# Two-layer convolution attention: half of layer 0's probability tiles turned by VectorE and DRAM instead of TensorE

## The chip, the cores and the metric

The kernel runs on one core of one Trainium2 chip. The metric is the device time of one execution in microseconds; the number given for a kernel is the median of its runs. Engines are named as in the profile: PE is TensorE, DVE VectorE, ACT ScalarE, POOL GpSimd, SP the SyncE that issues all DMAs here.

## The reference

Four images `x` of 256 channels and 32x32 = 1024 positions, all f32. Two layers:

```
# layer 0, per image; xf is (256, 1024)
Bm, Cm, Dm = Wb @ xf, Wc @ xf, Wd @ xf
S   = softmax(Bm.T @ Cm, axis=-1)          # 1024 x 1024
y   = gamma * (Dm @ S.T) + x
# layer 1, per image, 4 heads of 64 channels
hn  = group_norm(y, 32 groups) * g + b
q, k, v = Wq @ hn + bq, Wk @ hn + bk, Wv @ hn + bv
out = y + Wp @ (softmax(q.T @ k / 8) @ v, all heads) + bp
```

Products are made in split form: an operand is held as a rounded `_hi` part and the rest `_lo`, and a product is three matmuls (hi*hi, lo*hi, hi*lo), or two where one side is stacked.

## The kernel before

The instruction stream of every engine is written out by hand; semaphores join them. Each engine works strictly in its own order.

Layer 0 runs image by image: `image0(i, last)` on each engine, three times in a loop and once more written out for the last image (which also carries the group norm of layer 1's first image). `Wb.T @ Wc` is folded beforehand into `wbc`, so that `a = wbc.T x` and scores are `a.T x`. An image has 8 tiles of 128 queries (`T0_IMAGE = 8`), step s = 0..7. In a step:

- PE (`scores0`): 12 matmuls of 512 columns into `scores[:, s % 2]`. It waits until the exponential of tile s - 2 has left that buffer.
- DVE (`row_max`): the negated row maximum. ACT (`exp`): the exponential into `prob[:, s % 2]` and the row sum. DVE (`recip`), then POOL (`normalise`): the probabilities, in place in `prob`.
- Two steps later (`LAG = 2`) PE (`transpose_tile`) turns the tile: eight 128x128 transposes into the PSUM buffer `trans`, two halves of four. ACT (`trans_high`) copies each half rounded into `pt_hi`, DVE (`trans_low`) subtracts it from `trans` into `pt_lo`. There is one `trans` buffer, so a tile's transposes wait for `pt_lo` of the tile before (semaphore `pt_split`).
- In the steps of `D_STEPS` PE (`project_d`) also makes a quarter of Dm transposed, a "d product" of 12 matmuls of 256 columns, into one of two `acc` banks; ACT (`high`) and DVE (`low`) empty it into `d_hi`, `d_lo`. DVE does its part one step later, after that step's row maximum. A third d product needs the bank of the first, and so on.

After step 7 PE waits for the last d product to be emptied (`evacuated(plan.number("d3"))`) and starts the value products, `av0` to `av3`, 24 matmuls each. av0 and av1 need the turned tiles 0 to 3 (half 0 of `pt_hi`, `pt_lo`), av2 and av3 tiles 4 to 7. The list `TAIL0` sets what lies between: the transposes t6 and t7 and the next image's `a` products. The last image has `TAIL0_LAST`, with layer 1's first q and k products. SP loads `y_out` (the residual x) and the next image's `x_raw` at the start of an image, in the last image `y_in` in place of `x_raw`, and stores `y_out` in the tail.

Layer 1 has 32 tiles per image with the same helpers; its work does not change.

## Time and profile before

| | us |
|---|---|
| median of 3 runs | 707.8 (707.26 to 708.27) |
| the profiled execution | 707.9 |
| its span | 705.8 |
| PE busy | 697.6 |
| DVE busy | 536.4 |
| ACT busy | 454.3 |
| POOL busy | 229.4 |

The profile shows one execution. Layer 0 fills the span from about 16 to 265 us, some 62 us for each of its four images; before it stand the weights, behind it layer 1. An image's steps 0 to 7 take a little over half of its time, the tail the rest. Rows of the timeline give the start, the duration and the idle time ahead of an instruction with what ended it. A row's duration is a few hundredths of a microsecond, on PE 0.16, longer than the distance to the next row on the same engine, because instructions overlap at their ends; in sums over a queue the distance counts.

### The profile page before, as it was taken

Reading aid. Unit: us, or ns where it says so; the run is one execution under the profiler, and the core shown is the slowest. Engines: PE = TensorE matmul, PEld = TensorE weight load, DVE = VectorE, ACT = ScalarE, POOL = GpSimd, SP = SyncE. Lnnn points to the kernel's source line nnn. Section 1 sums busy time; section 2 is a strip of 40 time slices with the busy share of each in tenths; the row PEclk is TensorE's granted clock in tenths of the full one; section 3 lists DMA queues with packets and bytes.
Section 4 is the critical chain, followed back from the end, with each engine's and each line's share of the span. In section 5 each row is a group of like instructions: output and inputs, shape, how many; then the busy total and the mean of one; then the engine's idle time right before and its main releaser. Section 6 shows DMA issues by size and latency. Waiting matters only on the chain.

```text
span 705.8 us, 11728 instructions
## 1 busy us (share of the span) xinstructions
PE 697.6 (99%) x3924; PEld 595.8 (84%) x3924; DVE 536.4 (76%) x876; ACT 454.3 (64%) x820; POOL 229.4 (33%) x216
## 2 busy tenths in 40 slices
PE   8999999999999999999999999999999999999997
PEld 7888888888888888888888888888988888888886
DVE  4665365456547738899888899888889988889996
ACT  5552254145226516889777779777778878778884
POOL 0220121022013303466333446434356533334431
PEclk9999999999999999999999999999999999999999
DMA  8000310040030175500357301265401155401001
GB/s 276 8 2 38 101 41 15 30 134 0 31 127 22 43 182 125 160 1 1 76 135 176 93 31 31 53 158 134 134 15 45 45 124 123 126 16 46 1 31 59
DMA packets 29096, 52.69 MB, mean 75 GB/s; under 512 B 3456, under 2 KB 5760, under 8 KB 29056
## 3 DMA queue, kind: packets, MB, share of 16 engines
q1 hardware_dynamic: 29056, 52.19, 26.8%
q8 instruction: 21, 0.34, 0.2%
q14 instruction: 19, 0.16, 0.1%
HBM read 18.62 MB, written 8.39 MB: 38 GB/s over the span
## 4 chain that ended last, share of the span: by engine, by line
PE 91%; DVE 4%; ACT 3%; issue 1%; DMA 0%; DVEq 0%; SPq 0%; ACTq 0%
PE acc L1125 46%; PE scores L1125 27%; PE trans L1159 18%; DVE negmax L796 2%; ACT prob L601 1%; DVE pt_lo L814 1%; ACT pt_hi L611 1%; DMA wc_raw<-in_wc 0%; PE trans L1171 0%; DVE o_sum L1028 0%; DVE rsum L801 0%; ACT o_sum L717 0%; DVE y_res L1037 0%; DVE wb_lo L886 0%; DVE qk L931 0%
## 5 line engine op out<-in xcount | busy, mean ns | idle before, releaser
L510 POOL TENSOR_SCALAR prob<-prob,rsum 128x1024 f32<-128x1024 f32 x159 | 179.2, 1127 | 428.4 <-DVE rsum L801 428.4
L611 ACT ACTIVATE pt_hi<-trans 128x512 fp32r<-128x512 f32 x320 | 174.4, 595 | 129.1 <-PE trans L1159 128.6
L796 DVE TENSOR_REDUCE negmax<-scores 128x1 f32<-128x1024 f32 x160 | 194.3, 1214 | 44.3 <-PE scores L1125 43.3
L814 DVE TENSOR_TENSOR pt_lo<-trans,pt_hi 128x512 fp32r<-128x512 f32 x320 | 204.6, 680 | 7.0 <-ACT pt_hi L611 6.6
L601 ACT ACTIVATE prob<-scores,negmax 128x1024 f32<-128x1024 f32 x160 | 179.1, 1119 | 30.1 <-DVE negmax L796 28.5
L1159 PEld LDWEIGHTS trans<-ident,prob 128*128 128x128 f32 x1280 | 147.5, 140 | 26.8 <-issue 3.8
L1159 PE MATMUL trans<-ident,prob 128*128 128x128 f32 x1280 | 167.7, 273 | 1.3 <-DVE pt_lo L814 1.1
L1125 PE MATMUL scores<-k_st,q_st 128*128 128x512 f32 x512 | 137.7, 391 | 0.0
L1125 PEld LDWEIGHTS scores<-k_st,q_st 128*128 128x128 f32 x512 | 95.8, 188 | 20.4
L1125 PE MATMUL acc<-pt_hi,v_st 128*128 128x512 f32 (+1 forms) x264 | 106.8, 407 | 0.6 <-DVE pt_lo L814 0.6
L1125 PE MATMUL acc<-pt_lo,v_st 128*128 128x512 f32 (+1 forms) x264 | 101.0, 385 | 0.0
L1125 PEld LDWEIGHTS acc<-pt_hi,v_st 128*128 128x128 f32 x264 | 49.8, 189 | 7.8 <-DVE pt_lo L814 0.8
L1125 PEld LDWEIGHTS acc<-pt_lo,v_st 128*128 128x128 f32 x264 | 50.0, 189 | 7.1
L1125 PE MATMUL scores<-x_hi,a_hi 128*128 128x512 f32 x128 | 50.8, 397 | 0.0
L1125 PE MATMUL acc<-pt_hi,d_hi 128*128 128x512 f32 x128 | 50.7, 396 | 0.0
L1125 PE MATMUL scores<-x_hi,a_lo 128*128 128x512 f32 x128 | 50.0, 391 | 0.0
L1125 PE MATMUL scores<-x_lo,a_hi 128*128 128x512 f32 x128 | 49.9, 390 | 0.0
L1125 PE MATMUL acc<-pt_hi,d_lo 128*128 128x512 f32 x128 | 49.9, 390 | 0.0
L1125 PE MATMUL acc<-pt_lo,d_hi 128*128 128x512 f32 x128 | 49.9, 390 | 0.0
L801 DVE RECIPROCAL rsum<-rowsum 128x1 f32<-128x1 f32 x160 | 25.7, 161 | 27.0 <-ACT prob L601 22.3
L626 ACT ACTIVATE a_hi<-acc 128x512 fp32r<-128x512 f32 x16 | 9.6, 598 | 46.7 <-PE acc L1125 46.7
L945 DVE SCALAR_TENSOR_TENSOR y_out<-acc,vec,y_out 128x512 f32<-128x512 f32 x16 | 12.0, 750 | 27.6 <-PE acc L1125 27.6
(121 smaller groups left out, 892.7 us busy)
## 6 DMA issues: line engine op xcount, KB each, us to landing
k_st<-qk SPq DMA_DIRECT2D x64, 256.0 KB, 4.7
q_st<-qk SPq DMA_DIRECT2D x64, 128.0 KB, 2.4
x_raw<-in_x SPq DMA_DIRECT2D x8, 512.0 KB, 6.9
y_out<-in_x SPq DMA_DIRECT2D x16, 256.0 KB, 3.6
y_scratch<-y_out SPq DMA_DIRECT2D x16, 256.0 KB, 2.0
y_in<-y_scratch SPq DMA_DIRECT2D x4, 1024.0 KB, 7.2
y_res<-y_scratch SPq DMA_DIRECT2D x16, 256.0 KB, 3.8
out<-y_res SPq DMA_DIRECT2D x16, 256.0 KB, 2.1
```

The lines of the kernel that those rows point to most:

```text
L510: nc.gpsimd.tensor_scalar(p, p, rsum[:, t % 2:t % 2 + 1], 1.0, ALU.mult, ALU.mult)\
L601: nc.scalar.activation(prob[:, t % 2, :], scores[:, t % 2, :], ACT.Exp, bias=negmax[:, t % 2:t % 2 + 1], scale=1.0, accum_out=rowsum[:, t ...
L611: nc.scalar.activation(pt_block(pt_hi, (t // 4) % 2, t, h), trans[:, h, :].rearrange("p (j n) -> p j n", n=P), ACT.Copy).then_inc(pt_high, 1)
L626: nc.scalar.activation(dst, acc[:, plan.bank(name), :], ACT.Copy).then_inc(acc_high, 1)
L796: nc.vector.tensor_reduce(negmax[:, t % 2:t % 2 + 1], scores[:, t % 2, :], AX_X, ALU.max, negate=True).then_inc(max_ready, 1)
L801: nc.vector.reciprocal(rsum[:, t % 2:t % 2 + 1], rowsum[:, t % 2:t % 2 + 1]).then_inc(rsum_ready, 1)
L814: nc.vector.tensor_tensor(pt_block(pt_lo, slot, t, h), trans[:, h, :].rearrange("p (j n) -> p j n", n=P), pt_block(pt_hi, slot, t, h).bitc ...
L945: nc.vector.scalar_tensor_tensor(y_out[:, a, :], acc[:, plan.bank(f"av{a}"), :], vec[:, GAMMA:GAMMA + 1], y_out[:, a, :], ALU.mult, ALU.ad ...
L1125: ins = nc.tensor.matmul(dst, w, m, start=(starts and n == 0), stop=(stops and n == len(pairs) - 1))
L1159: ins = nc.tensor.transpose(trans[:, h, b * P:(b + 1) * P], prob[:, t % 2, j * P:(j + 1) * P], ident[:, :])
```

## The change

In layer 0, tiles 0 to 3 of every image (`TURNED = 4`) are no longer turned by PE. DVE (`turn`) transposes the normalised tile in 32x32 blocks from `prob` into one of three `turned` buffers, sorting the blocks by column on the way; SP stores it to DRAM (`store_turned`) and reads it back with the blocks of rows exchanged (`load_turned`, four DMAs of 32 rows), right into `pt_lo`. ACT (`turn_high_of`) then rounds the whole tile of 128x1024 from `pt_lo` into `pt_hi`, and DVE (`turn_low_of`) subtracts in place. Tiles 4 to 7 go as before. Half 0 of `pt_hi`, `pt_lo` now has another order of keys, which `turned_keys` gives to av0 and av1. The d products move from steps 1, 2, 4, 5 to 3, 4, 5, 6. The exponential of tiles 2 to 5 now waits for the turn of two tiles before instead of for PE's transposes. In step 4, DVE turns tile 3 ahead of the row maximum; in steps 1 to 3 the turn comes behind it.

The diff, cut; index changes of the semaphore counts (`TR_IMAGE`, `TR_SHIFT`) are left out:

```diff
-D_STEPS = [1, 2, 4, 5]
+D_STEPS = [3, 4, 5, 6]
+TURNED = 4
+TURN_SLOTS = 3
+TURN_HIGH = {4: [0], 5: [1, 2], 6: [3]}
+TURN_LOW = {4: [0], 5: [1], 6: [2, 3]}
...
 # SP, image0
+            def store_turned(i, t):
+                sp.wait_ge(turn_ready, TURNED * i + t + 1)
+                sp.dma_start(turn_dram[t], turned[:, t % TURN_SLOTS, :]).then_inc(turn_stored[t % TURN_SLOTS], 16)
+            def load_turned(i, t):
+                sp.wait_ge(turn_stored[t % TURN_SLOTS], turns_stored(i, t) + 16)
+                blocks = turn_dram[t].rearrange("(q c) (g n) -> g c q n", q=QUADS, g=QUADS)
+                for g in range(QUADS):
+                    rows = turned_tile(pt_lo, t).bitcast(F32)[g * QUAD:(g + 1) * QUAD, :]
+                    sp.dma_start(rows.rearrange("c (q n) -> c q n", q=QUADS), blocks[g]).then_inc(turn_moved[t], 16)
...
                     load_x(i + 1)
+                for t in range(TURNED):
+                    store_turned(i, t)
+                    if t > 0:
+                        load_turned(i, t - 1)
+                load_turned(i, TURNED - 1)
...
 # ACT, image0
+            def turn_high_of(i, t):
+                act.wait_ge(turn_moved[t], TURN_DMA * (i + 1))
+                nc.scalar.activation(turned_tile(pt_hi, t), turned_tile(pt_lo, t).bitcast(F32), ACT.Copy)\
+                    .then_inc(turn_high, 1)
...
                 for s in range(T0_IMAGE):
-                    if s >= LAG:
+                    if s >= LAG + TURNED:
                         trans(s - LAG)
-                    exp(t0, s)
+                    exp0(i, s)
...
                         high(d_part(d_hi, n), plan, f"d{n}")
+                    for t in TURN_HIGH.get(s, []):
+                        turn_high_of(i, t)
...
 # DVE, image0
+            def turn(i, t):
+                dve.wait_ge(prob_ready, T0_IMAGE * i + t + 1)
+                dve.wait_ge(turn_stored[t % TURN_SLOTS], turns_stored(i, t))
+                nc.vector.transpose(turned[:, t % TURN_SLOTS, :],
+                                    prob[:, t % 2, :].rearrange("p (j g c) -> p g j c", g=QUADS, c=QUAD))\
+                    .then_inc(turn_ready, 1)
+            def turn_low_of(i, t):
+                dve.wait_ge(turn_high, TURNED * i + t + 1)
+                nc.vector.tensor_tensor(turned_tile(pt_lo, t), turned_tile(pt_lo, t).bitcast(F32),
+                                        turned_tile(pt_hi, t).bitcast(F32), ALU.subtract).then_inc(turn_low, 1)
...
                         recip(t0, s - 1)
+                    if s == TURNED:
+                        turn(i, s - 1)
                     row_max(t0, s)
+                    if 1 <= s < TURNED:
+                        turn(i, s - 1)
                     if s - 1 in D_STEPS:
...
-                    if s >= LAG:
-                        trans_low(t0, s - LAG)
+                    if s >= LAG + TURNED:
+                        trans_low(TR_IMAGE * i - TURNED, s - LAG)
+                    for t in TURN_LOW.get(s, []):
+                        turn_low_of(i, t)
...
 # PE, image0
-                        pe.wait_ge(pt_split, SPLIT_CREDIT + 2 * t0 + 8 * (half + 1))
+                        if half == 0:
+                            pe.wait_ge(turn_low, TURNED * i + TURNED)
+                        else:
+                            pe.wait_ge(pt_split, SPLIT_CREDIT + 2 * TR_IMAGE * i + 2 * TR_IMAGE)
```

What stands in a row on the engines that wait for each other. First DVE in the loop over images, from the reciprocal that opens step 5, as it was (`exp_ready`, `scores_ready` and `acc_high` are the semaphores of the exponential, the scores and the d product's copy):

```order
L801 RECIPROCAL rsum<-rowsum 128x1 [waits exp_ready]
L796 TENSOR_REDUCE negmax<-scores 128x1 [waits scores_ready]
L897 REGISTER_ALU
L898 TENSOR_TENSOR d_lo<-acc,d_hi 128x512 [waits acc_high]
L812 ISA
L814 TENSOR_TENSOR pt_lo<-trans,pt_hi 128x4x128 [waits pt_high]
```

And now, steps 4 and 5:

```order
L870 RECIPROCAL rsum<-rowsum 128x1 [waits exp_ready]
L882 ISA [waits prob_ready]
L883 STREAM_TRANSPOSE turned<-prob 128x1024 [waits turn_stored0]
L865 TENSOR_REDUCE negmax<-scores 128x1 [waits scores_ready]
L980 REGISTER_ALU
L981 TENSOR_TENSOR d_lo<-acc,d_hi 128x512 [waits acc_high]
L889 ISA
L890 TENSOR_TENSOR pt_lo<-pt_lo,pt_hi 128x1024 [waits turn_high]
L870 RECIPROCAL rsum<-rowsum 128x1 [waits exp_ready]
L865 TENSOR_REDUCE negmax<-scores 128x1 [waits scores_ready]
```

The turn of tile 3 stands ahead of the maximum of step 4, and the subtraction of turned tile 0, which waits for ACT, ahead of the maximum of step 5.

ACT in step 4, before:

```order
L610 REGISTER_ALU
L611 ACTIVATE pt_hi<-trans 128x4x128 [waits transposed]
L599 REGISTER_ALU
L600 ISA [waits max_ready]
L601 ACTIVATE prob,rowsum<-scores,negmax 128x1024 [waits transposed]
L596 REGISTER_ALU
L626 ACTIVATE d_hi<-acc 128x512 [waits acc_done]
```

And now, in step 4 and at the start of step 5 (`turn_moved0` is counted up by the four loads of tile 0):

```order
L655 REGISTER_ALU [waits max_ready]
L668 ACTIVATE prob,rowsum<-scores,negmax 128x1024 [waits turn_ready]
L645 REGISTER_ALU
L693 ACTIVATE d_hi<-acc 128x512 [waits acc_done]
L663 ISA
L664 ACTIVATE pt_hi<-pt_lo 128x1024 [waits turn_moved0]
L653 REGISTER_ALU
L655 REGISTER_ALU [waits max_ready]
```

The copies out of `trans` ahead of the exponential are gone, and a copy of twice the width stands behind the d product's.

DVE from step 7 to the tail, before (`res_loaded` opens the tail's first result):

```order
L801 RECIPROCAL rsum<-rowsum 128x1 [waits exp_ready]
L796 TENSOR_REDUCE negmax<-scores 128x1 [waits scores_ready]
L812 ISA
L814 TENSOR_TENSOR pt_lo<-trans,pt_hi 128x4x128 [waits pt_high]
L812 REGISTER_ALU
L814 TENSOR_TENSOR pt_lo<-trans,pt_hi 128x4x128 [waits pt_high]
```

And now, from the end of step 6:

```order
L890 TENSOR_TENSOR pt_lo<-pt_lo,pt_hi 128x1024 [waits turn_high]
L870 RECIPROCAL rsum<-rowsum 128x1 [waits exp_ready]
L865 TENSOR_REDUCE negmax<-scores 128x1 [waits scores_ready]
L980 REGISTER_ALU
L981 TENSOR_TENSOR d_lo<-acc,d_hi 128x512 [waits acc_high]
L895 ISA
L897 TENSOR_TENSOR pt_lo<-trans,pt_hi 128x4x128 [waits pt_high]
```

The emptying of the last d product, for which PE waits ahead of av0, has come behind the maximum of step 7; it was in step 6.

## Rows read from the trace of the kernel before

**Rows 1.** Page, part 1: busy us, share of the span, instructions.

```profile
PE 697.6 (99%) x3924; PEld 595.8 (84%) x3924; DVE 536.4 (76%) x876; ACT 454.3 (64%) x820; POOL 229.4 (33%) x216
```

**Rows 2.** Timeline of PE, second image: start us, us, engine, line, what.

```profile
78.45 0.39 PE L1125 MATMUL scores<-x_hi,a_hi 128*128 128x512 f32 x1
...
83.89 0.28 PE L1125 MATMUL acc<-wd_hi,x_hi 128*128 128x256 f32 x1
...
85.32 0.40 PE L1125 MATMUL scores<-x_hi,a_hi 128*128 128x512 f32 x1
...
93.14 1.03 PE L1159 MATMUL trans<-ident,prob 128*128 128x128 f32 x8
...
96.75 1.03 PE L1159 MATMUL trans<-ident,prob 128*128 128x128 f32 x8
...
111.27 0.48 PE L1125 MATMUL acc<-pt_hi,d_hi 128*128 128x512 f32 x1
```

**Rows 3.** Timeline of DVE, the same image.

```profile
81.37 1.22 DVE L796 TENSOR_REDUCE negmax<-scores 128x1 f32<-128x1024 f32 x1 [1.40 <-PE scores L1125]
83.95 0.17 DVE L801 RECIPROCAL rsum<-rowsum 128x1 f32<-128x1 f32 x1 [1.35 <-ACT prob L601]
...
89.42 0.68 DVE L898 TENSOR_TENSOR d_lo<-acc,d_hi 128x512 fp32r<-128x512 f32 x1
90.01 1.28 DVE L814 TENSOR_TENSOR pt_lo<-trans,pt_hi 128x512 fp32r<-128x512 f32 x2
91.21 0.15 DVE L801 RECIPROCAL rsum<-rowsum 128x1 f32<-128x1 f32 x1
```

**Rows 4.** Timeline of ACT, the same image.

```profile
82.71 1.11 ACT L601 ACTIVATE prob<-scores,negmax 128x1024 f32<-128x1024 f32 x1 [3.46 <-DVE negmax L796]
...
89.68 1.12 ACT L601 ACTIVATE prob<-scores,negmax 128x1024 f32<-128x1024 f32 x1
...
90.77 0.61 ACT L626 ACTIVATE d_hi<-acc 128x512 fp32r<-128x512 f32 x1
```

**Rows 5.** Timeline of POOL, the same image.

```profile
91.56 1.12 POOL L510 TENSOR_SCALAR prob<-prob,rsum 128x1024 f32<-128x1024 f32 x1 [3.41 <-DVE rsum L801]
```

**Rows 6.** Groups by form: busy us, mean ns; idle before. All operands in SBUF.

```profile
L892 DVE TENSOR_TENSOR x_lo<-x_raw,x_hi 128x1024 fp32r<-128x1024 f32 x8 | 9.5, 1223 | 1.0 <-ACT x_hi L622 0.5
L622 ACT ACTIVATE x_hi<-x_raw 128x1024 fp32r<-128x1024 f32 x8 | 8.1, 1058 | 0.2 <-DMA x_raw<-in_x 0.2
L807 DVE TENSOR_SCALAR prob<-prob,rsum 128x1024 f32<-128x1024 f32 x1 | 0.8, 754 | 0.0
```

**Rows 7.** SP's issues, a window with DMA share and GB/s last, landing times.

```profile
81.09 1.94 SPq L423 DMA_DIRECT2D y_out<-in_x  x4
83.30 0.94 SPq L390 DMA_DIRECT2D x_raw<-in_x  x2
...
91.00:92.00 1.00, 1.00 (x7) 0.80 (x5) 0.36 (x2) 0.38 (x1) 0.44 (x1) 1.00 0.04 16
...
q_st<-qk SPq DMA_DIRECT2D x64, 128.0 KB, 2.4
```

**Rows 8.** Timelines of PE, POOL, ACT and DVE in the last image.

```profile
202.26 0.39 PE L1125 MATMUL scores<-x_hi,a_hi 128*128 128x512 f32 x1
...
235.57 0.48 PE L1125 MATMUL acc<-pt_hi,d_hi 128*128 128x512 f32 x1
...
212.12 1.35 POOL L538 TENSOR_TENSOR gn_root<-gn_var,minus_half 128x6 f32<-128x6 f32 x1
...
223.74 0.64 ACT L661 ACTIVATE h_hi<-y_in 128x512 fp32r<-128x512 f32 x1
...
215.51 0.29 DVE L868 TENSOR_TENSOR gn_scale<-gn_root,vec 128x2 f32<-128x2 f32 x3
...
228.05 0.68 DVE L355 TENSOR_TENSOR h_lo<-y_in,h_hi 128x512 fp32r<-128x512 f32 x1
```

**Rows 9.** Timeline of PE at the program's start.

```profile
1.81 4.64 PE L1171 MATMUL trans<-ident 128*128 128x128 f32 x20 [1.81 <-POOL ident L490]
```

More of the change, by code:

```diff
@@ L53 @@
 FIRST_A = ["a0", "a1", "a2", "a3"]
-D_STEPS = [1, 2, 4, 5]
+D_STEPS = [3, 4, 5, 6]
+TURNED = 4
+TR_IMAGE = T0_IMAGE - TURNED
+TR_SHIFT = IMAGES * TURNED
+QUAD = 32
+QUADS = P // QUAD
+TURN_SLOTS = 3
+TURN_DMA = QUADS * 16
+TURN_HIGH = {4: [0], 5: [1, 2], 6: [3]}
+TURN_LOW = {4: [0], 5: [1], 6: [2, 3]}
 TAIL0 = ["av0", "t6", ("av1", 0, 2), "t7", ("av1", 1, 2), "av2", "next_a0", ("av3", 0, 3), "next_a1",
@@ L315, in build @@
         transposed = sem("transposed")
+        turn_ready = sem("turn_ready")
+        turn_stored = [sem(f"turn_stored{n}") for n in range(TURN_SLOTS)]
+        turn_moved = [sem(f"turn_moved{n}") for n in range(TURNED)]
+        turn_high = sem("turn_high")
+        turn_low = sem("turn_low")
         pt_high = sem("pt_high")
@@ L363, in flat, with turned_tile, turned_keys, turns_stored @@
             return ap.rearrange("p a b -> p (a b)")
+        def turned_tile(buf, t):
+            return buf[:, 0, :, :].rearrange("p j n -> p (j n)")[:, t * N:(t + 1) * N]
+        def turned_keys(buf, j):
+            return buf[:, 0, :, :].rearrange("p j n -> p (j n)").rearrange("p (m j c) -> p m j c", j=NT, c=QUAD)[:, :, j, :]
+        def turns_stored(i, t):
+            return FREE_CREDIT + 16 * (2 * i + t // TURN_SLOTS if t % TURN_SLOTS == 0 else i)
         def pt_block(buf, half_slot, t, h):
@@ L381, in _ @@
         def _(sp):
-            for s in (y_stored, out_stored, *qk_stacked):
+            for s in (y_stored, out_stored, *qk_stacked, *turn_stored):
                 sp.sem_inc(s, FREE_CREDIT)
@@ L599, in exp, with exp0, exponential @@
                 act.wait_ge(max_ready, t0 + t + 1)
-                act.wait_ge(transposed, TRANS_CREDIT + 2 * (t0 + t) - 2)
+                act.wait_ge(transposed, TRANS_CREDIT + 2 * (t0 - TR_SHIFT + t) - 2)
+                exponential(t)
+            def exp0(i, t):
+                act.wait_ge(max_ready, T0_IMAGE * i + t + 1)
+                if 2 <= t < 2 + TURNED:
+                    act.wait_ge(turn_ready, TURNED * i + t - 1)
+                else:
+                    tiles = TR_IMAGE * i + (t - TURNED if t >= 2 + TURNED else t)
+                    act.wait_ge(transposed, TRANS_CREDIT - 2 + 2 * tiles)
+                exponential(t)
+            def turn_high_of(i, t):
+                act.wait_ge(turn_moved[t], TURN_DMA * (i + 1))
+                nc.scalar.activation(turned_tile(pt_hi, t), turned_tile(pt_lo, t).bitcast(F32), ACT.Copy)\
+                    .then_inc(turn_high, 1)
+            def exponential(t):
                 nc.scalar.activation(prob[:, t % 2, :], scores[:, t % 2, :], ACT.Exp,
@@ L609, in trans_high @@
                 for h in range(2):
-                    act.wait_ge(transposed, TRANS_CREDIT + 2 * (t0 + t) + h + 1)
+                    act.wait_ge(transposed, TRANS_CREDIT + 2 * (tr + t) + h + 1)
                     nc.scalar.activation(pt_block(pt_hi, (t // 4) % 2, t, h),
@@ L669, in trans @@
                     before = BASES["layer0"] + len(LAYER0) * (i - 1) + LAYER0.index("av3" if t >= 4 else "av1")
-                    trans_high(t0, t, before)
+                    trans_high(TR_IMAGE * i - TURNED, t, before)
                 for s in range(T0_IMAGE):
-                    if s >= LAG:
+                    if s >= LAG + TURNED:
                         trans(s - LAG)
-                    exp(t0, s)
+                    exp0(i, s)
                     if last and s - 1 in NORM_STEPS0:
@@ L766, in image1 @@
                         evacuate(plan, head_outputs(STEPS1[s]), i)
-                    trans_high(t1, s, before)
+                    trans_high(t1 - TR_SHIFT, s, before)
                     if s + LAG < T1_IMAGE or not plan.last:
@@ L1148, in over_k, with transpose_tile @@
                         for pair in products((w(0, k), m(0, k)), (w(1, k), m(1, k)))]
-            def transpose_tile(t0, t, last=False):
+            def transpose_tile(t0, tr, t, last=False):
                 if last and t >= T1_IMAGE - DVE_TILES:
@@ L1249, in values @@
                     if ct == 0 and part == 0:
-                        pe.wait_ge(pt_split, SPLIT_CREDIT + 2 * t0 + 8 * (half + 1))
+                        if half == 0:
+                            pe.wait_ge(turn_low, TURNED * i + TURNED)
+                        else:
+                            pe.wait_ge(pt_split, SPLIT_CREDIT + 2 * TR_IMAGE * i + 2 * TR_IMAGE)
+                    keys = (lambda buf, j: buf[:, 1, j, :]) if half else turned_keys
                     group(plan, f"av{n}", [
                         pair for j in range(NT)
-                        for pair in products((d_hi[:, j, col(ct, P)], pt_hi[:, half, j, :]),
-                                             (d_lo[:, j, col(ct, P)], pt_lo[:, half, j, :]))],
+                        for pair in products((d_hi[:, j, col(ct, P)], keys(pt_hi, j)),
+                                             (d_lo[:, j, col(ct, P)], keys(pt_lo, j)))],
                         part=part, parts=parts)
@@ L1374, in image1 @@
                         side_values(0, 0, 2)
-                    transpose_tile(t1, s, plan.last)
+                    transpose_tile(t1, t1 - TR_SHIFT, s, plan.last)
                     if not (plan.first and s == 0) and not groups_first:
```

25 lines of the change are left out of this document (13 added, 12 removed).

## Prediction

> **What bounds the kernel now.** I read the busy times first: PE is busy for 697.6 of 705.8 us, DVE for 76% and ACT for 64% [rows 1]. So what counts is which PE work goes, and whether DVE and ACT, now comfortably behind PE, can keep up where they get more. Then I read one image of layer 0 on PE [rows 2]: the reader is to see that its groups follow each other without a gap. Two score groups fill 78.45 to 83.89, so one takes 2.72 us; a d product takes 1.43 (83.89 to 85.32); from one tile's transposes to the next is 3.61 (93.14 to 96.75), which less 2.72 leaves 0.90 for the eight transposes of a tile. The first value matmul starts at 111.27, 32.8 us after the image's first score matmul. I call that stretch the head of an image and count its times from 78.45. Since PE never waits in it before, any change shows as the new start of av0 against 32.8; what follows av0 keeps its order, paced by PE. Last I read DVE, ACT and POOL in the same stretch for the hand-overs [rows 3 to 5]: scores done to row maximum 0.20 (81.17 to 81.37); maximum to exponential 1.34 (81.37 to 82.71); exponential to reciprocal 1.24 (82.71 to 83.95); reciprocal to POOL 0.35 (91.21 to 91.56), where normalising takes 1.12; exponential to the next ACT instruction 1.09 (89.68 to 90.77); d_lo 0.59 and a pt_lo pair 1.20 on DVE's queue (89.42, 90.01, 91.21). A PE that has run dry needs about 0.2 more to load weights. With these numbers the head before comes out at 32.9 by hand, the trace says 32.8.
>
> **What goes from PE.** Tiles 0 to 3 of each of four images lose 8 transposes: 4 x 0.90 = 3.6 us an image, 14.4 in all. If nothing else bound, the time would be 707.9 - 14.4 = 693.5.
>
> **The first steps, scores only.** With d products moved from steps 1, 2, 4, 5 to 3, 4, 5, 6, score groups 0 to 3 stand back to back. scores(2) needs exp(0): 2.72 + 0.20 + 1.34 + 1.24 + 0.23 = 5.73 against 5.44 when PE is free, so 0.3 us of waiting; scores(3) then just fits.
>
> **The turn on DVE.** The trace has no block transpose. Nearest rows of 128x1024 f32: 0.75 for the in-place scale from SBUF, 1.22 for the x_lo subtraction [rows 6]; a maximum over the same elements is 1.22 too [rows 3]. I take 1.22, or 1.14 on the queue, since an operation that moves every element once has no reason to be at the fast row's pace; I keep 0.75 and 2.44 (two passes) as ends. A step of DVE in this stretch is then recip 0.15 + max 1.14 + turn 1.14 = 2.4, which fits 2.72. But turn(3) is placed ahead of max(4): exp(3) starts at 12.7, recip(3) at 14.0, POOL works 14.3 to 15.4, turn(3) 15.5 to 16.7, so max(4) starts at 16.7, where scores(4) had been done at 15.5. That alone costs PE nothing, which has d(1), scores(5) and d(2) to do.
>
> The Trainium skill gives two figures here. "VectorE: DVE Perf Modes", The three transpose paths, has 311 ns for 128x128 on VectorE, by which eight blocks would be some 2.5 us, an estimate; "Vector Engine (DVE) Microarchitecture Reference", The reshape front-end and per-opcode configuration, says that a transpose sustains one element per cycle per lane, which is the pace of the rows at 1.22. No row here shows the operation; by the first figure the sum would be that of the first rival.
>
> **The hand-over that takes PE's place.** From step 4 on, each DVE step ends in turn_low, which waits for turn_high on ACT, which stands behind exp and d_hi of the same step, which wait for this step's maximum. The next maximum stands behind turn_low. So DVE and ACT go in a ring: max to exp 1.34, exp 1.09, d_hi 0.52, turn_high 1.09 (x_hi, same shape and source, 1.06 [rows 6]), turn_low 1.14 (x_lo, 1.22), recip 0.15: 5.33 us a step. PE needs 2.72 + 1.43 = 4.15 a step. Hence max(5) at 22.0, max(6) at 27.3. In step 6 DVE's own queue is the longer: max 1.14, d_lo(2) 0.60, pt_lo(4) 1.20, turn_low(2) and (3) 2.28, recip 0.15 = 5.37, so max(7) at 32.7. Only then comes d_lo(3), done at 34.5, and PE waits for it ahead of av0 (evacuated(d3)): av0 at 34.8. PE alone would have been there at 32.8 - 3.6 + 0.3 = 29.5. So 3.6 us of transposes go and 5.5 us of waiting come: in two pieces, some 2 us ahead of the transposes of tile 5 (their buffer waits for pt_lo(4)) and some 3 us ahead of av0. Net **+1.9 us** an image.
>
> **The round trip.** SP issues the store of a tile and later four loads; two x_raw issues take 0.94 and four y_out issues 1.94, so some 2 us of SP for a tile's four loads [rows 7]. The x loads of the next image are ahead in the same queue and still fill the DMA until about 91, 12.6 on our count; the window behind it is empty [rows 7]. Store(0), issued at 8.4, would land at 14 to 14.5, its loads be issued by 16.3 and land (128 KB: 2.4 us) near 18.7; turn_high(0) is due at 19.6. The later three have 2 to 4 us to spare. turn(3) also needs slot 0, stored by 14.5, due 15.5. So I cost the round trip at nothing, hidden behind exp(4) and the wait for POOL, with 1 us of cover; every microsecond that it is later than that is one on the ring. The y and x issues that follow on SP lie far ahead of need.
>
> **The last image** has group norm work in the same queues [rows 8]: the root on POOL (1.35) and the affine step on DVE (three rows of 0.29 at 0.33 apart and a copy, 1.1) now lie between turn(1) and recip(2), with no d product under them: max(4) comes 1.4 later. h_hi stands between exp and d_hi in steps 4 and 5: 2 x 0.52. h_lo stands in DVE's step 6: 0.60. Its head before was itself 33.3 (202.26 to 235.57), not 32.8: 0.5 less. 1.9 + 1.4 + 1.0 + 0.6 - 0.5 = **+4.4**.
>
> **Sum.** 3 x 1.9 + 4.4 = +10.1 us. The profiled execution took 707.9 us (span 705.8 and 2.1 around it), the median of the runs is 707.8; 707.9 + 10.1 = 718.0. Ends of the unknown: a turn of 0.75 takes some 0.4 off an image (716.5); 0.2 less on turn_high and turn_low together take off 0.6 (715.5); a round trip 1 us past its cover adds 1 (722), 3 us add 3 (some 728 to 730).
>
> **Rivals.** (A) *The turn takes two passes, 2.44.* Then DVE itself sets steps 1 to 3: recip 0.15 + max 1.43 with the wait for POOL + turn 2.36 = 3.94 a step, max(4) moves to 21.3 and the head by 6.5 us: 707.9 + 4 x 6.5 + 2.5 = about 736. Against it stand the rows at 1.22. (B) *DVE and ACT keep up, so that the kernel is faster.* Place: the ring of steps 4 to 6. It decides at the point where av0 can start by 32.8, 1.9 earlier than I have it: three turns of the ring at 4.7 instead of 5.33. If turn_high and turn_low went at half my durations each turn would lose 1.1 and the head would end at about 31.4: 707.9 - 4 x 1.4 + 2.5 = about 705; with the ring gone altogether 707.9 - 14.4 + 1.2 = 694.7. For it speaks that DVE is busy for only 76% of the span and ACT for 64% [rows 1]; against it that this is a chain of waits, not a load. (C) *The round trip is late.* Stores and loads share DMA queues with 2 MB of x traffic; if tile 0 lands 1 to 3 us after 19.6, 722 to 730. (D) *PE's clock falls in the pauses.* PE would stand for some 2 and 3 us with a short burst between. At the program's start 20 matmuls of 128 columns took 0.232 each, those of a transposed tile 0.13 [rows 9, 2]: the lower level costs as much again. If it held through av0 (5.4 us) that is at most 5.4 more an image, 739; I would give half of it, 728. No stretch of the trace has pauses of this size, for or against.
>
> **Chances.** Forecast 0.58 (715 to 721), A 0.10, B 0.09, of which two thirds beat the old kernel by over 0.2% and a third lies within it, C 0.17, D 0.06. The range takes in the forecast, most of C and D and the mild part of A: 713 to 729. Within 0.2% (1.4 us, about what a measurement of this kernel tells from no change) 0.03, faster 0.06, slower 0.91.
>
> **What would show it.** PE waits ahead of av0 for d_lo, about 3 us in each image, and ahead of tile 5's transposes about 2; DVE waits for turn_high about 2.3 us twice an image; maxima 4, 5, 6 of an image 5.3 apart; PE's busy time falls by some 14 us plus what is modelled in pauses; the block transpose has a row near 1.2. Wrong if ACT waits for the load of tile 0 (C), if transposes last over 1.5 (A), if the granted clock falls below 1.00 in a head (D), or if maxima come at PE's 4.15 (B).

## The result, and the profile after

The changed kernel takes 726.5 us (median of 4 runs, 725.53 to 727.14) against 707.9 (707.26 to 708.27) for the kernel before: 1.026 times as long, 95% interval 1.0252 to 1.0277. The direction was as forecast, and the time lies within the range of 713 to 729, but 8.5 us above the forecast of 718.0. The experiments are mostly about these 8.5 us.

The profiled execution took 727.1 us, with a span of 725.4 against 705.8. From the page of the changed kernel come the busy times, to be held against [rows 1], the row of PE's granted clock (tenths of full speed in 40 slices), one group of matmuls (busy us, mean ns, idle before it), and two rows of DMA issues (count, KB each, us from issue to landing):

```profile
PE 696.2 (96%) x3796; PEld 587.5 (81%) x3796; DVE 553.7 (76%) x876; ACT 453.7 (63%) x804; POOL 229.5 (32%) x216
...
PEclk9989999999899999999999999999999999999999
...
L1214 PE MATMUL acc<-pt_hi,d_hi 128*128 128x512 f32 x128 | 55.3, 432 | 14.9 <-DVE d_lo L981 14.9
...
turn_scratch<-turned SPq DMA_DIRECT2D x16, 512.0 KB, 4.4
pt_lo<-turn_scratch SPq DMA_DIRECT2D x64, 128.0 KB, 3.7
```

128 transposes are gone from PE, yet its busy time fell by only 1.4 us, not by the 14 that they took and that the prediction named as a sign. That is the first sign that the matmuls that stayed have become slower.

To find where the time is, I cut each image in two at the start of its first value matmul (av0). The head, as in the prediction, runs from the image's first score matmul to av0; I call what follows, up to the next image's first score matmul (or, behind the last image, layer 1's), the tail. All numbers are differences of start times on PE's timeline.

| us | image 0 | 1 | 2 | 3 | sum |
|---|---|---|---|---|---|
| head before | 32.82 | 32.82 | 32.82 | 33.31 | 131.8 |
| head after | 34.80 | 35.02 | 34.64 | 37.02 | 141.5 |
| tail before | 29.08 | 29.09 | 29.08 | 30.70 | 118.0 |
| tail after | 31.84 | 30.96 | 32.13 | 33.19 | 128.1 |

The heads grew by 9.7 us, where 10.1 was forecast. The tails, costed at nothing, grew by 10.2. What lies ahead of the first image became 0.4 shorter; its end stands between 16.0 and 16.9 us in the ten traces of this document, so 0.4 is within what it varies by. Layer 1's first score matmul comes 19.5 later (266.27 before, 285.76 after), and the span is 19.6 longer: layer 1 is untouched.

The second image's head, as DVE's and ACT's timelines show it (start us, us, engine, line, what; in brackets the idle time before it and who ended it):

```profile
98.38 1.25 DVE L883 STREAM_TRANSPOSE turned<-prob 128x1024 f32<-128x1024 f32 x1 [1.48 <-POOL prob L559]
99.54 1.19 DVE L865 TENSOR_REDUCE negmax<-scores 128x1 f32<-128x1024 f32 x1
...
103.56 1.23 DVE L890 TENSOR_TENSOR pt_lo<-pt_lo,pt_hi 128x1024 fp32r<-128x1024 f32 x1 [2.24 <-ACT pt_hi L664]
...
104.78 1.21 DVE L865 TENSOR_REDUCE negmax<-scores 128x1 f32<-128x1024 f32 x1
...
108.77 1.23 DVE L890 TENSOR_TENSOR pt_lo<-pt_lo,pt_hi 128x1024 fp32r<-128x1024 f32 x1 [2.19 <-ACT pt_hi L664]
...
109.98 1.21 DVE L865 TENSOR_REDUCE negmax<-scores 128x1 f32<-128x1024 f32 x1
...
115.79 1.21 DVE L865 TENSOR_REDUCE negmax<-scores 128x1 f32<-128x1024 f32 x1
116.92 0.68 DVE L981 TENSOR_TENSOR d_lo<-acc,d_hi 128x512 fp32r<-128x512 f32 x1
```

```profile
102.47 1.06 ACT L664 ACTIVATE pt_hi<-pt_lo 128x1024 fp32r<-128x1024 f32 x1
...
109.99 1.06 ACT L664 ACTIVATE pt_hi<-pt_lo 128x1024 fp32r<-128x1024 f32 x1 [1.25 <-DMA pt_lo<-turn_scratch]
```

The four maxima (tiles 4 to 7) stand 5.24, 5.20 and 5.81 us apart. Between the first two pairs DVE stands 2.2 us for ACT's half of the turned tile, which itself could start only behind this step's exponential. This is the ring of the prediction. Here is what it does to PE at the end of the head and just behind it; the windows under it hold, after the times, the busy us of PE, PEld, DVE, ACT and POOL, then the granted clock (third number from the end):

```profile
112.44 1.25 PE L1248 MATMUL trans<-ident,prob 128*128 128x128 f32 x8 [0.73 <-DVE pt_lo L897]
117.82 0.79 PE L1214 MATMUL acc<-pt_hi,d_hi 128*128 128x512 f32 x1 [4.12 <-DVE d_lo L981]
118.41 0.63 PE L1214 MATMUL acc<-pt_hi,d_lo 128*128 128x512 f32 x1
118.83 0.63 PE L1214 MATMUL acc<-pt_lo,d_hi 128*128 128x512 f32 x1
```

```profile
113.00:114.00 1.00, 0.70 (x5) 0.42 (x4) 1.00 (x1) 1.00 (x4) 0.00 (x0) 1.00 0.00 0
...
117.00:118.00 1.00, 0.18 (x1) 0.18 (x2) 1.00 (x2) 0.89 (x1) 0.20 (x1) 0.76 0.00 0
118.00:119.00 1.00, 1.00 (x3) 0.82 (x4) 0.86 (x3) 0.32 (x2) 0.00 (x0) 0.50 0.00 0
120.00:121.00 1.00, 1.00 (x4) 0.73 (x4) 0.00 (x0) 0.00 (x0) 0.18 (x1) 0.53 0.00 0
121.00:122.00 1.00, 1.00 (x6) 0.80 (x5) 0.00 (x0) 0.00 (x0) 0.00 (x0) 1.00 0.00 0
```

PE is still at its full 2.4 GHz (clock 1.00) when the pause of 4.12 us begins, and near its end the granted clock falls to 0.50, the 1.2 GHz level. When av0 starts, its matmuls of 512 columns follow each other at 0.42 to 0.43 us instead of 0.23. At about 121 the clock is back. In images 0, 2 and 3, with pauses of 3.57, 3.81 and 3.40 us ahead of av0, the granted clock is at 0.50 when av0 starts, too, and is back at about 56, 189 and 257 us, 5 to 6 us behind that start.

My theory after this reading had three parts: the heads are the ring and the late d_lo; most of the tails is the clock after the pause; and what is left of the tails is something in the matmuls themselves, since also at full clock they start 0.237 to 0.24 apart instead of 0.227. The rivals were that the tails are slow because data arrive late (the round trip, or POOL and DVE behind it), and that the heads wait for the round trip rather than for the ring.

### The profile page after: what moved, and what is told of

Its sections match the earlier page's. It is cut to its first block, busy times and chain, and to the rows that moved or that the text cites. A ratio compares the mean times of both kernels' runs of the same rounds, so it can differ in the third digit from the quotient of the medians.

```text
span 725.4 us, 11499 instructions
## 1 busy us (share of the span) xinstructions
PE 696.2 (96%) x3796; PEld 587.5 (81%) x3796; DVE 553.7 (76%) x876; ACT 453.7 (63%) x804; POOL 229.5 (32%) x216
## 4 chain that ended last, share of the span: by engine, by line
PE 74%; DVE 9%; ACT 5%; issue 5%; DMA 4%; POOL 1%; SPq 1%; DVEq 0%; ACTq 0%; POOLq 0%
PE acc L1214 43%; PE scores L1214 16%; PE trans L1248 15%; DVE negmax L865 4%; DMA turn_scratch<-turned 3%; ACT prob L668 2%; DVE pt_lo L897 1%; DMA pt_lo<-turn_scratch 1%; ACT pt_hi L678 1%; POOL prob L559 1%; SPq L461 1%; ACT pt_hi L664 1%; DVE turned L883 1%; DVE pt_lo L890 1%; DVE rsum L870 0%
## 5 line engine op out<-in xcount | busy, mean ns | idle before, releaser
L678 ACT ACTIVATE pt_hi<-trans 128x512 fp32r<-128x512 f32 x288 | 157.0, 595 | 99.8 <-PE trans L1248 99.3
L897 DVE TENSOR_TENSOR pt_lo<-trans,pt_hi 128x512 fp32r<-128x512 f32 x288 | 184.2, 681 | 10.8 <-ACT pt_hi L678 10.4
L1248 PEld LDWEIGHTS trans<-ident,prob 128*128 128x128 f32 x1152 | 132.3, 140 | 32.0 <-issue 6.5
L1248 PE MATMUL trans<-ident,prob 128*128 128x128 f32 x1152 | 152.0, 274 | 6.4 <-DVE pt_lo L897 5.5
L1214 PE MATMUL acc<-pt_hi,d_hi 128*128 128x512 f32 x128 | 55.3, 432 | 14.9 <-DVE d_lo L981 14.9
L1214 PE MATMUL acc<-pt_hi,d_lo 128*128 128x512 f32 x128 | 53.7, 420 | 0.0
L1214 PE MATMUL acc<-pt_lo,d_hi 128*128 128x512 f32 x128 | 53.4, 417 | 0.0
L1214 PEld LDWEIGHTS acc<-pt_hi,d_hi 128*128 128x128 f32 x128 | 26.3, 206 | 21.6 <-DVE d_lo L981 15.8
```

Of the source, the lines that this page charges most:

```text
L678: nc.scalar.activation(pt_block(pt_hi, (t // 4) % 2, t, h), trans[:, h, :].rearrange("p (j n) -> p j n", n=P), ACT.Copy).then_inc(pt_high, 1)
L897: nc.vector.tensor_tensor(pt_block(pt_lo, slot, t, h), trans[:, h, :].rearrange("p (j n) -> p j n", n=P), pt_block(pt_hi, slot, t, h).bitc ...
L1214: ins = nc.tensor.matmul(dst, w, m, start=(starts and n == 0), stop=(stops and n == len(pairs) - 1))
L1248: ins = nc.tensor.transpose(trans[:, h, b * P:(b + 1) * P], prob[:, t % 2, j * P:(j + 1) * P], ident[:, :])
```

## Experiment 1: give PE work in the pause

Where the image's PE program comes to its wait for the last d_lo, 12 matmuls are put in. They write into a score buffer that nobody reads any more.

```diff
+                pe.wait_ge(exp_ready, t0 + T0_IMAGE + 1)
+                for _ in range(12):
+                    nc.tensor.matmul(scores[:, 0, 0:H], a_hi[:, 0, 0:P], x_hi[:, 0, 0:H], start=True, stop=True)
```

> The changed kernel with 12 extra matmuls of 512 columns (2.7 us at full rate) that PE makes in the pause ahead of av0 into the scores buffer of tile 6, which nobody reads any more. The heads of the images (first score matmul to av0) should stay at 34.8 to 37.0 us. Theory 1 (about half of the loss, 10.2 of 19.5 us, is the granted clock that falls in the pause and comes back only inside av0 and av1): the granted clock stays at 1.00, the stretches from av0 to the next image's scores return from 31 to 32 us to 29.1, and the kernel takes 726.5 - 10.2 = 716 us. Rival (the values are slow for another reason, such as the other order of keys in their operands): the stretches stay at 31 to 32 us and the kernel at 726.

Measured: 718.9 us (718.47 to 719.23; 1.0155 times the kernel before on that chip, 1.0138 to 1.0172), 7.6 less than the change. PE's timeline of the second image:

```profile
111.47 3.01 PE L1375 MATMUL scores<-x_hi,a_hi 128*128 128x512 f32 x12
115.29 0.50 PE L1214 MATMUL acc<-pt_hi,d_hi 128*128 128x512 f32 x1 [0.81 <-DVE d_lo L981]
115.62 0.40 PE L1214 MATMUL acc<-pt_hi,d_lo 128*128 128x512 f32 x1
115.86 0.40 PE L1214 MATMUL acc<-pt_lo,d_hi 128*128 128x512 f32 x1
```

More work on PE makes the kernel faster. In sum the heads are what they were (34.79, 34.37, 34.38 and 37.82), so nothing arrives earlier; the tails fall to 29.57, 29.56, 29.56 and 30.91. The clock is thus worth 8.5 us of the tails (128.12 less 119.60), and late data none of them. Still 1.65 above the tails before remain, in matmuls 0.24 apart. They are the larger part of the 3 us by which 719 is above what I had expected; most of the rest is the last image's head of 37.8. Here is why it is longer than the 37.0 of the change, a row of PE's timeline and a window of the last image:

```profile
242.25 4.52 PE L1375 MATMUL scores<-x_hi,a_hi 128*128 128x512 f32 x12
...
243.00:244.00 1.00, 1.00 (x4) 0.81 (x3) 1.00 (x3) 0.23 (x1) 0.00 (x0) 0.50 0.00 0
```

In this image PE had already stood for 2.36 us ahead of the transposes of tile 5, and just behind them the granted clock fell to 0.50. The 12 extra matmuls took 4.4 us instead of the 2.9 of the second image, and av0 (246.61) had to wait for them. So the filler did not keep the clock up everywhere; here it took the slow stretch in av0's place.

## Experiment 2: turn_low a step later

If DVE waits for turn_high because it follows too closely, let it come one step later:

```diff
-TURN_LOW = {4: [0], 5: [1], 6: [2, 3]}
+TURN_LOW = {5: [0, 1], 6: [2, 3]}
```

> The changed kernel with the subtractions of turned tiles 0 and 1 one step later, so that TURN_LOW is 5: 0, 1 and 6: 2, 3; nothing else. Theory 1 (the ring of DVE and ACT: maximum, exponential, d copy, turned copy, subtraction, next maximum): maxima 4, 5, 6 come at PE's pace, the head falls from 34.8 to about 32.8 us, the pause ahead of av0 to under 3 us, and with it the clock stays up more often: 708 to 713 us. Rival (DVE is simply full from step 4 on, or PE waits for the late d copy whatever the order): the work on DVE is the same, so the head stays within 0.5 of 34.8 and the kernel at 724 to 727 us.

Measured: 719.6 us (718.99 to 720.69; 1.0171, 1.0154 to 1.0188), 7 less than the change but 7 to 12 more than I expected. In the first image the head falls to 32.6, as the theory of the ring says. In the second and third it is 34.3 and 34.4, only 0.8 and 0.3 less than in the change: here ACT waits for the turned tile itself, for 2.6 and 2.7 us of 6.6 in all. In the last it falls from 37.0 to 34.4. The clock accounts for much of the rest of the miss: it stays at 1.00 over the 2.42 us that PE stands ahead of av0 in the first image, and falls to 0.50 in the other three (4.25, 4.25 and 3.40 us), whose tails are 31.1, 30.8 and 33.7. The first row is from the list of waits (us in total, times, longest us), the second from ACT's timeline of the second image.

```profile
ACT pt_hi L664 <- DMA pt_lo<-turn_scratch: 6.6, 4, 2.7
...
105.49 1.06 ACT L664 ACTIVATE pt_hi<-pt_lo 128x1024 fp32r<-128x1024 f32 x1 [2.58 <-DMA pt_lo<-turn_scratch]
```

So with the ring loosened the round trip takes its place in the second and third image, less than 2 us behind it. The prediction's "hidden, with 1 us of cover" was right about the change and says nothing for a kernel that is 2 us quicker there.

## Experiment 3: the d products late, and nothing else

On the kernel before, only the steps of the d products are moved; all tiles are still turned by PE.

```diff
-D_STEPS = [1, 2, 4, 5]
+D_STEPS = [3, 4, 5, 6]
```

> The kernel before with only the d products moved to steps 3, 4, 5, 6; no tile is turned by DVE. Theory 1: d_lo(3) stands behind the maximum of step 7 and PE waits for it ahead of av0 by some 1.6 us an image, too short for the clock to fall: 707.9 + 4 x 1.6 = 714 us. Rival (the late d products are hidden and only the turned tiles cost): 708 us, within 1. A third: the pause brings the clock down here too: 720 us or more.

Measured: 714.7 us (714.20 to 715.42; 1.0100, 1.0083 to 1.0117), as expected; the heads are 34.5 to 34.9. Rows from DVE's and PE's timelines of the second image:

```profile
112.49 1.22 DVE L796 TENSOR_REDUCE negmax<-scores 128x1 f32<-128x1024 f32 x1 [1.97 <-PE scores L1125]
113.63 0.68 DVE L898 TENSOR_TENSOR d_lo<-acc,d_hi 128x512 fp32r<-128x512 f32 x1
```

```profile
114.53 0.49 PE L1125 MATMUL acc<-pt_hi,d_hi 128*128 128x512 f32 x1 [1.21 <-DVE d_lo L898]
114.86 0.40 PE L1125 MATMUL acc<-pt_hi,d_lo 128*128 128x512 f32 x1
```

The move costs 6.5 us by itself: the last d_lo stands behind the last maximum on DVE, and av0 waits for it. There is a pause ahead of av0 here too, of 1.21 us, and the granted clock stays at 1.00, with matmuls at the usual distance.

## Experiment 4: a new order of the steps

This keeps all that the change does and reorders it: the first d product back at step 1, the last at 5, turn_high early and turn_low late, and each turn behind the maximum of its step in tile 4's step too.

```diff
-D_STEPS = [3, 4, 5, 6]
+D_STEPS = [1, 3, 4, 5]
...
-TURN_HIGH = {4: [0], 5: [1, 2], 6: [3]}
-TURN_LOW = {4: [0], 5: [1], 6: [2, 3]}
+TURN_HIGH = {4: [0, 1], 5: [2], 6: [3]}
+TURN_LOW = {5: [0, 1], 6: [2, 3]}
...
-                    if s == TURNED:
-                        turn(i, s - 1)
...
-                    if 1 <= s < TURNED:
+                    if 1 <= s <= TURNED:
```

> The changed kernel in another order: d products in steps 1, 3, 4, 5, the turn of tile 3 behind the maximum of step 4, turned copies on ACT in steps 4 (tiles 0, 1), 5 (2), 6 (3), subtractions on DVE in steps 5 (0, 1) and 6 (2, 3). Theory 1: no ring, no maximum behind a subtraction that waits, d_lo(3) in step 6. By the same sum as in the prediction the head is 30.5 to 31.8 us, so 1.0 to 2.3 less than before an image, PE's pause under 2 us, the clock stays up: 699 to 705 us, faster than both kernels. Rival (the round trip through DRAM is the bound once the ring is gone): ACT waits for the loads in step 4, the head is 33 us or more and the kernel at 708 or above.

Measured: 708.5 us (706.57 to 709.88, 10 runs; 1.0003, 0.9993 to 1.0013). That is 18 us less than the change and no different from the kernel before, above the 699 to 705 that I expected and at the rival's time. In the first image the head is 30.8; in the others 32.3 to 32.7. First the row from the list of waits and one from ACT's timeline, then two from PE's and one window, all of the second image but the first:

```profile
ACT pt_hi L664 <- DMA pt_lo<-turn_scratch: 10.9, 8, 2.5
...
99.61 1.06 ACT L664 ACTIVATE pt_hi<-pt_lo 128x1024 fp32r<-128x1024 f32 x1 [2.27 <-DMA pt_lo<-turn_scratch]
```

```profile
105.74 1.25 PE L1246 MATMUL trans<-ident,prob 128*128 128x128 f32 x8 [0.46 <-DVE pt_lo L897]
108.88 0.50 PE L1212 MATMUL acc<-pt_hi,d_hi 128*128 128x512 f32 x1 [1.89 <-DVE pt_lo L890]
...
110.00:111.00 1.00, 1.00 (x4) 0.78 (x3) 1.00 (x2) 0.94 (x1) 0.15 (x1) 0.50 0.00 0
```

The maxima of tiles 4 to 6 start at 93.35, 97.53 and 101.92, so 4.2 and 4.4 us apart, close to PE's 4.15 a step: the ring is gone. The 18 us were thus the order, and now the round trip is what ACT waits for, 8 times. SP's issues show why the first image, with a head of 30.8, fares better:

```profile
12.43 0.95 SPq L421 DMA_DIRECT2D x_raw<-in_x  x2
25.19 3.65 SPq L453 DMA_DIRECT2D turn_scratch<-turned  x2
28.98 2.20 SPq L461 DMA_DIRECT2D pt_lo<-turn_scratch  x4
...
79.26 1.93 SPq L467 DMA_DIRECT2D y_out<-in_x  x4
81.46 0.94 SPq L421 DMA_DIRECT2D x_raw<-in_x  x2
85.12 4.08 SPq L453 DMA_DIRECT2D turn_scratch<-turned  x2
91.64 1.74 SPq L461 DMA_DIRECT2D pt_lo<-turn_scratch  x4
```

There the next image's x is issued 4 us ahead of the first score matmul (16.27), 12.8 ahead of the first store; in the second image the y and x loads are issued 3 to 5 us behind it (76.63), right ahead of the store. SP issues tile 0's loads behind the stores of tiles 0 and 1 (the `x2` rows), and only once store 0 has landed. In the first image they follow at once, 3.8 us behind store 0; in the second they come 2.4 us after the row of the stores ends, 6.5 behind store 0. The window above shows the clock at 0.50 behind pauses of 0.46 and 1.89 us with eight transposes between them. In the third image of the same execution, with 0.51 and 1.89 us at the same places, it stayed at 1.00, and the tail is 29.6 instead of 31.1. I had expected the clock to stay up with pauses under 2 us; it did so in some images only.

## Experiments 5 and 6: the other loads behind the round trip

SP issues the four y_out loads and the x loads of the next image behind the turned tiles' stores and loads, not ahead of them. Experiment 5 does this to the changed kernel, experiment 6 to that of experiment 4.

```diff
-                for a in range(4):
-                    sp.dma_start(y_out[:, a, :], x[i, a % 2, :, (a // 2) * H:(a // 2 + 1) * H]).then_inc(res_loaded, 16)
...
-                else:
-                    sp.wait_ge(x_split, X_HALVES * (i + 1))
-                    load_x(i + 1)
...
+                for a in range(4):
+                    sp.dma_start(y_out[:, a, :], x[i, a % 2, :, (a // 2) * H:(a // 2 + 1) * H]).then_inc(res_loaded, 16)
+                if not last:
+                    sp.wait_ge(x_split, X_HALVES * (i + 1))
+                    load_x(i + 1)
```

> The changed kernel with SP's loads of y_out and of the next image's x_raw issued behind the stores and loads of the turned tiles instead of ahead of them; the order of the other engines is as in the changed kernel. Theory 1 (in the changed kernel the ring of DVE and ACT binds and the round trip is hidden, but for 0.2 us in one image): the heads stay at 34.6 to 37.0 us and the kernel at 726, within 2. Rival (the round trip behind the x loads is what sets the heads): they fall by 1 us or more an image and the kernel to 722 or less.

> The new order of e4_new_order (708.5 us, heads 30.8, 32.3, 32.3, 32.7) with the loads of y_out and x_raw behind the turned tiles. Theory 1 (in e4 the ring is gone and the round trip binds in images 1 to 3, because 2 MB of loads stand ahead of it): ACT's waits for turned tiles go, heads 30.8 in images 0 to 2 and 32 in the last, pauses of about 1.2 us so that the clock stays up, and 708.5 - 3 x 1.5 - 0.6 - 1.5 to 3.3 of clock = 700 to 702 us, faster than the kernel before. Rival (the round trip's own latency and SP's issues bind, not the traffic ahead of it): heads stay above 32 and the kernel at 707 or more.

Measured for 5: 726.3 us (724.88 to 728.21; 1.0253, 1.0221 to 1.0285), as expected the same as the change. Its list of waits no longer has ACT waiting for the turned tiles at all; the heads are 34.8, 34.4, 34.4 and 37.0, in sum 0.9 less than those of the change. So in the change's profiled execution the round trip is worth 1 us at most. In experiment 1, with the loads still ahead, the second and third head are 34.4 as well, so even this much differs from execution to execution.

Measured for 6: **705.1 us** (703.60 to 706.34, 9 runs; ratio 0.9958, 0.9943 to 0.9973), faster than either kernel. The same edit that gave nothing at 5 gives 3.3 us here (between two chips, on which the kernel before differed by 0.4). A row of the list of waits, SP's first store and loads of the second image, and av0 in the second and third image on PE's timeline:

```profile
ACT pt_hi L664 <- DMA pt_lo<-turn_scratch: 8.5, 9, 1.3
...
85.64 4.07 SPq L453 DMA_DIRECT2D turn_scratch<-turned  x2
89.84 2.18 SPq L461 DMA_DIRECT2D pt_lo<-turn_scratch  x4
...
107.95 0.50 PE L1212 MATMUL acc<-pt_hi,d_hi 128*128 128x512 f32 x1 [1.27 <-DVE pt_lo L890]
...
168.51 0.50 PE L1212 MATMUL acc<-pt_hi,d_hi 128*128 128x512 f32 x1 [1.47 <-DVE pt_lo L890]
```

The loads of tile 0 now follow right behind the second store, 4.2 us behind the first instead of 6.5. The profiled execution is one of the two fastest (703.7 us, the granted clock at 1.00 throughout). Its heads are 31.3, 30.8, 31.0 and 32.7, in sum 6.0 below those of before, and the tails 2.3 above them; with the 0.3 won ahead of the first image that makes 3.9, and the span fell from 705.8 to 702.0. Against the trace of experiment 4 the heads are 2.2 us shorter and the tails 2.5. That kernel's clock fell in two images of its trace, so a part of the 3.3 us between the two medians is clock and not the loads; how large a part, the two traces don't say.

I had expected 700 to 702 for the time, with ACT's waits gone. They are not: 8.5 us of 10.9 remain, though only the last image still has a load ahead of its stores (`y_in`). What remains in the other three is the round trip's own length, the mechanism of the rival, if not its times. PE stands for 1.3 to 2.0 us ahead of av0. Of the 14.4 us that left PE, the heads keep 6.0 and the kernel's median 2.6.

## Experiment 7: what the turned tiles' layout costs

The block transposes leave the keys of a turned tile in another order, and av0 and av1 read them in runs of 32 elements. On the kernel before, one half of the queries is read that way; nothing else changes.

```diff
+                    keys = (lambda buf, j: buf[:, 1, j, :]) if half else (
+                        lambda buf, j: buf[:, 0, :, :].rearrange("p j n -> p (j n)")
+                        .rearrange("p (m j c) -> p m j c", j=NT, c=32)[:, :, j, :])
...
-                        for pair in products((d_hi[:, j, col(ct, P)], pt_hi[:, half, j, :]),
-                                             (d_lo[:, j, col(ct, P)], pt_lo[:, half, j, :]))],
+                        for pair in products((d_hi[:, j, col(ct, P)], keys(pt_hi, j)),
+                                             (d_lo[:, j, col(ct, P)], keys(pt_lo, j)))],
```

> The kernel before, in which av0 and av1 read their moving operand (pt_hi, pt_lo, half 0) in 16 runs of 32 elements instead of one run of 512, as the turned tiles are read; it multiplies keys in the wrong order and does nothing else otherwise. In e1_warm, at full granted clock, the 48 matmuls of av0 and av1 take 0.237 us each instead of 0.227, 0.49 us an image. Theory (the runs of 32 cost that): tails of 29.57 instead of 29.08 us and 707.9 + 4 x 0.49 = 709.9 us. Rival (it is an after-effect of the pause or of DVE and ACT reading beside it): tails stay at 29.08 and the kernel at 708.

Measured: 709.4 us (709.02 to 711.28, 10 runs; 1.0020, 1.0008 to 1.0032). The heads are those of before to 0.01 us; the tails are 29.54 three times and 31.09, in all 1.8 longer. The matmuls of av0, on PE's timeline:

```profile
111.60 0.40 PE L1125 MATMUL acc<-pt_hi,d_lo 128*128 128x512 f32 x1
...
112.55 0.40 PE L1125 MATMUL acc<-pt_lo,d_hi 128*128 128x512 f32 x1
```

They start 0.2375 apart (111.60 to 112.55, four of them); in the kernel before the score matmuls of an image start 0.227 apart (24 of them from 78.45 to 83.89 [rows 2]). 48 of them an image at 0.0105 more are 0.5 us; the tails are 0.4 to 0.5 longer. In sum this is the part of the tails that experiment 1 left (1.8 here, 1.65 there).

## Experiment 8: the d products early again

The changed kernel with `D_STEPS = [1, 2, 4, 5]`, the steps of the kernel before.

> The changed kernel with the d products back in steps 1, 2, 4, 5; tiles 0 to 3 still turned by DVE and DRAM. Theory 1 (the ring binds, and two steps later d products ahead of it only delay the maxima): the maximum of step 4 comes 2.9 us later than in the changed kernel, PE waits inside the steps for exponentials and for tile 4's probabilities, and the head is 35.5 to 36 us, so 1 us more than in the changed kernel; the pauses are more and shorter, so less clock is lost: 722 to 730 us. Rival (the change loses only because d_lo(3) is late): the head falls to 33 us or less and the kernel to 712 or less.

Measured: 730.1 us (730.07 to 730.67; 1.0302, 1.0278 to 1.0327), as expected at the upper end. The heads are 35.5 three times and 37.7. I had also expected less clock to be lost, and that did not come: the tails are 128.6 in sum, as in the change (128.1). The maxima of tiles 4 to 7 in the second image, whose first score matmul is at 83.75:

```profile
103.42 1.19 DVE L865 TENSOR_REDUCE negmax<-scores 128x1 f32<-128x1024 f32 x1
...
108.60 1.21 DVE L865 TENSOR_REDUCE negmax<-scores 128x1 f32<-128x1024 f32 x1
...
113.81 1.20 DVE L865 TENSOR_REDUCE negmax<-scores 128x1 f32<-128x1024 f32 x1
...
119.06 1.20 DVE L865 TENSOR_REDUCE negmax<-scores 128x1 f32<-128x1024 f32 x1
```

The ring enters at 19.7 us (103.42 less 83.75) and not at 16.7, and then turns at the same 5.2 a step. So the late d products of the change, which cost 6.5 us by themselves, are the better choice beside this ring: they let it start 3 us earlier, and of that the kernel gives part back in the wait for the last d_lo. No late d_lo stands in these heads (PE waits for pt_lo ahead of av0), and they are 144.1 in sum, 12.3 above those of before: the ring takes back more than the transposes gave also without it.

## Why the prediction was right and where it was wrong

The direction came true, and the time lies in the range. But half of the added time is in terms that the forecast left out, and the range held them only because it had been drawn wide enough for rivals C and D. The mechanism of the heads was right; that the whole came out inside the range owes something to luck.

**The turn on DVE: right.** I took 1.22 us. The 16 block transposes took these (minimum, median and maximum in ns):

```profile
L883 DVE STREAM_TRANSPOSE turned<-prob x16: 1233/1245/1247, 23.8 to 232.1; 128x1024 f32<-128x1024 f32 x16
```

Rival A, two passes, falls with it. Of the two figures of the Trainium skill, one element per cycle and lane ("Vector Engine (DVE) Microarchitecture Reference", The reshape front-end and per-opcode configuration) agrees with this row, which takes as long as a maximum over as many elements of a lane (1.21). Eight times the 311 ns of "VectorE: DVE Perf Modes", The three transpose paths, would be twice what was measured; the page gives that figure for bf16, which the prediction left out, and the tile here is f32.

**The ring and the late d_lo: right, in place and size.** The fifth maximum (tile 4) was forecast 16.7 us behind the image's start and came at 16.74 (99.54 less 82.80). The spacings were forecast as 5.33, 5.33 and 5.37 and measured as 5.24, 5.20 and 5.81. Without the round trip's wait (experiment 5) the third is 5.26, somewhat under the 5.37 that I had for DVE's own queue. av0 was forecast at 34.8 and came at 34.6 to 35.0; in the last image 37.0 for 37.7. The two waits of PE were split otherwise than I said: 0.7 us ahead of tile 5's transposes instead of 2, and 4.1 ahead of av0 instead of 3. That this is a ring and not DVE's or ACT's load is shown by experiments 2 and 4: the same instructions in another order take the first image's head to 32.6 and to 30.8, and the maxima of tiles 4 to 6 to PE's pace. Rival B thus did not come true for the change; a better order of the same work, with the loads moved, reached 705.1.

**The round trip: right that it is hidden, with less room than I thought.** Experiment 5 takes ACT's wait for it away and gains nothing that can be told from the change's own time. Tile 0's store was forecast to land 14 to 14.5 us behind the image's start; SP could issue the loads behind it at 15.2 (98.03 less 82.80). The one place where it shows in the second image is the wait of 1.25 us at 109.99, which makes the third spacing 5.81; the third image has one of 0.94. Rival C would have been next in line, as experiments 2 and 4 show.

**The clock: the term that was missing, and the step that failed.** The forecast had PE's pauses and their lengths, and then let av0 run at full speed. Rival D held just this, and its sign came true: the granted clock fell in the head of every image. Its price of 728 is close to the 726.5 measured, though it had 10.8 us for the clock, where 8.5 were measured, and nothing for the layout. I gave it 0.06 because no stretch of the trace before had such a pause, for or against. Where the trace can't say, 0.06 was too low: PE never rests in the kernel before, so the trace could not have shown the fall. The size that I gave, half of what a whole av0 at 0.50 would cost, was 2.7 us an image; measured are 2.3, 1.4, 2.6 and 2.3 (tails after less those of experiment 1), 8.5 in all. The price of the lower level I had taken from [rows 9], and that reading was unsound: these 20 are f32 matmuls of the identity with itself, not transposes, and in the windows of that stretch the granted clock is 1.00. The factor of about two came true all the same, 0.42 to 0.43 us against 0.2375 in av0.

**The layout: a term that I did not see.** The change alters how av0 and av1 read their operand, and I costed what follows av0 as "keeps its order, paced by PE". The order it kept; each matmul of av0 and av1 became 0.0105 us longer, 1.8 us in all (experiment 7).

**The sum.** Forecast +10.1: heads +9.7 measured. Not forecast: clock +8.5 and layout +1.7, which make the tails' +10.2. Ahead of the first image -0.4. Together +19.5, against 19.6 of the span. That the median lies 8.5 us above the forecast and the clock also took 8.5 is chance: the profiled execution is 9.4 above what was forecast for the parts, which is the clock and the layout less 0.4 of the heads and 0.4 ahead of the first image.

The clock's price per image goes with how long PE works at 0.50. From the start of av0 that is 5.1, 3.1, 5.8 and 4.9 us in images 0 to 3, and somewhat under half of each is what its tail lost (2.3, 1.4, 2.6, 2.3). What stays open is why the lower level lasts longer in one image than in another, and why it comes behind the same pauses in one image and not in the next (experiment 4).

The second image's head can be added up as well, though the prediction's own numbers (29.2 of work, 4.85 of waits) fall 1 us short of 35.0. An idle time in brackets counts from the end of a row, which on PE is 0.16 late, so the two waits are worth 5.2 and not 4.85. The transposes behind the first wait take 1.1 us and not 0.9, score groups 0 to 3 take 11.16 (82.80 to 93.96) and not 10.88, with the small wait that the prediction had at 0.3, and the four later groups and the last d product a little more than before.

## What to carry to other kernels

Where an edit makes PE stand for some microseconds in a kernel in which it never stood, price the matmuls behind the pause as well, or give it filler work and look whether the clock then holds (experiment 1: in three images of four); the trace of before can't show that cost. Before work is moved off the bounding engine, follow the step's loop through the engines that take it over: here 14.4 us left PE, and a ring of waits between two engines that were busy for two thirds to three quarters of the time took back more. Once the order is mended, look at what the moved data queue behind, since the same edit of the DMA order was worth nothing before that and 3.3 us after.
